# The first load of a fused cross-attention kernel as two DMAs of 64 partitions, issued by SyncE and by ScalarE

## What is computed

```python
B, C1, C2, N = (8, 512, 512, 1024)
D = C2 // 8
q = jnp.einsum('bcn,dc->bnd', x1, Wq) + bq
k = jnp.einsum('bcn,dc->bdn', x2, Wk) + bk[:, None]
v = jnp.einsum('bcn,dc->bdn', x2, Wv) + bv[:, None]
attn = jax.nn.softmax(jnp.einsum('bnd,bdm->bnm', q, k), axis=2)
attn_out = jnp.einsum('bcm,bnm->bcn', v, attn)
return attn_out + x1
```

## Time and profile before

| What | Value |
|---|---|
| Device time, median of 3 runs | 642.52 us (642.16 to 642.61) |
| Device time of the profiled execution | 642.35 us |
| Its span, first to last instruction | 640.6 us |
| Around the span | 1.75 us |
| Busy: PE, PEld, DVE, ACT, POOL | 636.6, 522.3, 461.2, 342.1, 120.6 us |
| DMA traffic | 100.11 MB, all but a few packets on SP's queue |

### The profile page before, as it was taken

The page is one execution under the profiler, slowest core; times in us unless marked ns, Lnnn a source line. Parts: engine busy times, 40 slices in busy tenths (PEclk is TensorE's granted clock), DMA queues, the critical chain, the costliest instruction groups (busy, mean ns, idle before and its releaser), DMA issues.

```text
span 640.6 us, 9766 instructions
## 1 busy us (share of the span) xinstructions
PE 636.6 (99%) x3522; PEld 522.3 (82%) x3522; DVE 461.2 (72%) x533; ACT 342.1 (53%) x451; POOL 120.6 (19%) x58
## 2 busy tenths in 40 slices
PE   9999999999999999999999999999999999999998
PEld 7888888888888888888888888888888888888886
DVE  6996769847698477994678946888558886498441
ACT  6786546734457445475455653555626647276120
POOL 0343100530006300062000620006200152002100
PEclk9999999999999999999999999999999999999999
DMA  8634435862267732776328753287442963434442
GB/s 339 200 135 102 127 105 146 308 171 87 90 166 278 180 95 69 189 266 168 98 65 220 255 147 101 79 232 249 126 126 73 257 224 106 131 94 119 109 146 73
DMA packets 40063, 100.11 MB, mean 156 GB/s; under 512 B 7280, under 2 KB 7536, under 8 KB 40048
## 3 DMA queue, kind: packets, MB, share of 16 engines
q1 hardware_dynamic: 40048, 99.91, 51.9%
HBM read 51.64 MB, written 16.78 MB: 107 GB/s over the span
## 4 chain that ended last, share of the span: by engine, by line
PE 99%; DMA 1%; DVE 0%; issue 0%
PE acc_ps L1154 43%; PE acc_ps L1132 15%; PE acc_ps L1185 10%; PE acc_ps L1122 9%; PE s_ps L1072 8%; PE s_ps L1088 7%; PE acc_ps L1335 2%; PE acc_ps L1320 1%; PE acc_ps L1203 1%; PE s_ps L1311 1%; DMA pt_raw<-in_head_dram 1%; PE acc_ps L1169 1%; PE acc_ps L1326 0%; PE acc_ps L1305 0%; PE s_ps L1080 0%; PE s_ps L1081 0%
## 5 line engine op out<-in xcount | busy, mean ns | idle before, releaser
L1154 PE MATMUL acc_ps<-pt_hi,vt_hi 128*128 128x512 f32 x408 | 158.9, 390 | 0.0
L1154 PE MATMUL acc_ps<-pt_hi,vt_lo 128*128 128x512 f32 x408 | 158.8, 389 | 0.0
L1154 PE MATMUL acc_ps<-pt_lo,vt_hi 128*128 128x512 f32 x408 | 158.8, 389 | 0.0
L362 POOL TENSOR_TENSOR pt_lo<-pt_raw,pt_hi 128x1024 fp32r<-128x1024 f32 x14 | 39.6, 2826 | 361.3 <-ACT pt_hi L426 361.3
L1154 PEld LDWEIGHTS acc_ps<-pt_hi,vt_hi 128*128 128x128 f32 x408 | 76.6, 188 | 16.2 <-issue 0.4
L1154 PEld LDWEIGHTS acc_ps<-pt_lo,vt_hi 128*128 128x128 f32 x408 | 76.6, 188 | 15.9
L1154 PEld LDWEIGHTS acc_ps<-pt_hi,vt_lo 128*128 128x128 f32 x408 | 76.6, 188 | 15.8
L776 DVE TENSOR_REDUCE negmax<-s_ps 128x1 f32<-128x1024 f32 x64 | 77.5, 1213 | 16.7 <-PE s_ps L1090 15.9
L362 POOL TENSOR_TENSOR xs_lo<-stage,xs_hi 128x1024 fp32r<-128x1024 f32 x29 | 71.9, 2501 | 82.0 <-ACT xs_hi L426 82.0
L525 ACT ACTIVATE probs<-s_ps,negmax 128x1024 f32<-128x1024 f32 x56 | 62.5, 1117 | 44.1 <-DVE negmax L776 43.6
L426 ACT ACTIVATE pt_hi<-pt_raw 128x1024 fp32r<-128x1024 f32 x60 | 61.9, 1057 | 27.3 <-PE acc_ps L1154 26.3
(11 more groups left out here) (173 smaller groups left out, 1422.1 us busy)
## 6 DMA issues: line engine op xcount, KB each, us to landing
pt_raw<-blocks SPq DMA_DIRECT2D x240, 128.0 KB, 2.3
stage<-in_x_dram SPq DMA_DIRECT2D x32, 512.0 KB, 6.8
o_sb<-in_x_dram SPq DMA_DIRECT2D x64, 256.0 KB, 3.4
out_dram<-o_sb SPq DMA_DIRECT2D x63, 256.0 KB, 2.4
stage<-in_ctx_dram SPq DMA_DIRECT2D x28, 512.0 KB, 9.1
pt_raw<-in_head_dram SPq DMA_DIRECT2D x4, 512.0 KB, 5.7
stage<-in_tail_dram SPq DMA_DIRECT2D x2, 512.0 KB, 7.4
v_sum<-in_wkq_dram SPq DMA_DIRECT2D x1, 256.0 KB, 4.9
```

What stands on the lines that cost most here:

```text
L362: return nc.gpsimd.tensor_tensor(out, src, hi.bitcast(F32), ALU.subtract)
L1154: mm = nc.tensor.matmul(acc_ps[:, out_bank(c, first), :], v[:, m, cols], p[:, m, :], start=(m == 0 and v is vt_hi and p is pt_hi), stop=(m ...
```

## The change

The first load, `head(0)`, becomes two DMAs. SP issues the one for partitions 0 to 63, ACT the one for partitions 64 to 127, as the first instruction of its own program. Both add 16 to the same semaphore, and the two engines that read the tile, ACT and DVE, wait for 32 in place of 16. All else stays.

```diff
@@ block.sync
-            head(0)
+            sp.dma_start(heads[0:D, 0, :], head_d[0, 0:D, :]).then_inc(s_head[0], 16)
             head(1)
             sp.dma_start(v_sum[:], wkq_d).then_inc(s_wkq, 16)
             tail(0)
@@ block.scalar
-            act.wait_ge(s_head[0], 16)
+            nc.scalar.dma_start(heads[D:2 * D, 0, :], head_d[0, D:2 * D, :]).then_inc(s_head[0], 16)
+            act.wait_ge(s_head[0], 2 * 16)
             copy(wv_hi[:, 0, 0:C // 2], wv_raw[:, 0, 0:C // 2]).then_inc(s_wvhi, 1)
             copy(xs_hi[:, 0, P:NH], head_raw[:, 0, P:NH]).then_inc(s_headhi, 1)
@@ block.vector
             def first_hi():
-                dve.wait_ge(s_head[0], 16)
+                dve.wait_ge(s_head[0], 2 * 16)
```

## The result

The changed kernel takes 643.63 us (median of 9 runs, 643.37 to 645.16) against 642.73 us for the kernel before (9 runs, 642.16 to 643.07). The ratio, which takes in all the runs, is 1.0023 with a 95% interval of 1.0015 to 1.0031; the medians alone differ by 0.14%. So the change is slower, by about the 0.2% that the prediction called detectable, and its time lies outside the predicted range, which ended at 643.3.

The account below looks back on a forecast made before the run. PE bounds the kernel, busy 636.6 of 640.6 us, so its start on real data sets the end. SP's half, ACT's half, table load, shared queues and waits each added 0: 642.5 us, range 642.0 to 643.3.

Parts of the forecast that it names:

- the rival that put it first: ACT's opening: table load stays ahead of ACT's issue, half lands 1.28 us late, 643.8 us or more; chance 0.09.
- ACT's half: First load: ACT's added issue moves the last byte by -0.10 to +0.34 us; value taken 0.
- two queues on the same engines: First load on the DMA engines: both queues served in turn, the second half ends when the single load ended; 0.
- one behind the other: First load: ACT's DMA is prepared after SP's and comes 0.43 us later, 642.95 us; chance 0.17.
- matmuls further apart only beside a clock under 1.00: PE behind its first real matmul: a sign that would show the forecast wrong; no size given.
- two floors: PE's start: at most 0.26 us earlier because of the zero matmuls, 0.18 us because of POOL's copy of k.

Follow-up runs that it names:

- two column halves, switch on: The changed kernel with halves cut by columns over all 128 partitions, `nc.dge_precook` left on, against the kernel before: 642.84 us, ratio 1.0006.
- the same, switch off: Column halves of 128 partitions issued by SP and ACT, with `nc.dge_precook` turned off for both loads: 642.90 us in its one run.

## Why the prediction was wrong

The sum of the delay, from the profiles of the kernels with one semaphore (us; "last packet" is the start of the last of the tile's closing packets):

| Kernel | last packet | tile complete | between | DVE starts | adds |
|---|---|---|---|---|---|
| one load (before) | 3.79 | 4.21 | 0.42 | 4.23 | |
| two column halves, switch on | 3.84 | 4.36 | 0.52 | 4.39 | 0.16 |
| the same, switch off | 4.46 | 4.77 | 0.31 | 4.79 | 0.40 |
| two halves of 64 partitions (the change) | 4.34 | 5.28 | 0.94 | 5.30 | 0.51 |

So the delay of 1.07 us has two parts of nearly equal size: the bytes end 0.55 us later, and the landing comes another 0.52 us later behind them. The first is about what the column halves lose with the switch off (0.67 us in their row), with the same issue times and ACT's bytes first. That it has the same cause in the 64-partition halves is my estimate from these numbers: no run turns the switch for them. The second comes with the cut into blocks of partitions: it isn't there with the column halves, switch on or off, nor with even and odd partitions, and it is there in every profile of the 64-partition halves (0.77 us and more) and, smaller, at the cut at 96. Single profiles differ by 0.2 us and more in the time of the bytes, so the first part is good to no more than that; the second is well outside its spread (0.94 to 1.02 in the change and its relatives).

**Right.** PE's start sets the end, one for one: 1.07 us later at the start, 1.0 in the span. No other wait of PE appeared. The table load stood behind the issue and was hidden, so the rival that put it first didn't happen. Where it did come late, in the kernels with two waits, its 1.28 us stood on the path as that rival said.

**Wrong: the term "ACT's half", -0.10 to +0.34 us, and "two queues on the same engines", 0.** They are the term that was mis-sized, and it measures +1.07. Three assumptions went into it. The issue was taken from a load of 128 partitions, 0.43 us; it is 0.56 to 0.59. The halves were to be served in turn; SP's first byte came 0.9 us behind ACT's. And the bounds were those of the issue alone. The prediction had counted 2.1 us outside the transfer, "the issue, the wait for the first byte and the report of the last one", and then let only the first of the three move. All three moved: alone, the first byte comes 1.37 and 1.78 us after the start of the issue for the halves of 64 partitions, against 1.02 and 0.97 for column halves with the switch on, and the report of the last one takes 0.94 us in the change against 0.42. The rival "one behind the other" had a part of the mechanism, with the order reversed (SP's half was the late one) and 0.43 us as its price; the late report, half of the delay, is in no rival.

**The row I should have read** is one of the moves between partitions. Besides two biases of a few bytes they are the only transfers of the kernel before that take a part of the partitions. It is the same in both kernels; here from the one after (ns, min/median/max):

```profile
L290 SPq DMA_DIRECT2D pt_raw<-blocks x240: 507/591/1940, 56.1 to 609.6; - x120
```

I bounded the issue by a store over all 128 partitions, 0.33 us, and by a bias of a few bytes, 0.77, and centred it on the loads, 0.43. The nearest row in shape says 0.59 for 32 partitions with 128 KB, half the bytes of a 64-partition half. It would have given the issue (0.56 to 0.59), but neither of the two larger parts.

**Wrong: the clock's part.** The clock column reads 1.00, and the prediction names matmuls further apart only beside a clock under 1.00, among what would show it wrong. That column can't be read so at the start, as shown at the end of this document. The one room its sums leave for a slower PE is the "or more" of the table-load rival, which neither a row nor a run gives a size there; the runs showed 1.5 us. With a gap of 1.3 us, three runs of nine cost 1.5 us more. It is an amount above the 1.0 us, not a separate case, and should have widened the upper end for every way in which the load lands late.

What stays open: why the halves of 64 partitions are issued in 0.56 to 0.59 us with the switch on, like column halves with it off (0.55 to 0.60), when 96 and 32 partitions take 0.40 and 0.33, why the landing of a block of partitions comes so late behind its last packet, and why SP's bytes come behind ACT's though its issue starts 0.01 us earlier. In 4.0 to 4.4 us SP's packets of the changed kernel also took nearly twice as long for their bytes (0.08 MB fill the engines to 98.5%, against 0.16 MB at 107% before); why isn't known.

No version beat both kernels. The whole tile alone on the engines landed 0.2 us sooner in its one profile, but by the prediction's two floors, 0.26 and 0.18 us, there is too little to win for a measurement to show it.

## What to carry to other kernels

Where an engine is busy to the end, the first load is paid one for one (here 1.07 us at PE's start, 1.0 us in the span), and splitting it in two is a gamble on the times before the first byte and behind the last, which half the size didn't halve here: alone they were 1.03 and 0.36 us for the whole tile, 1.02 and 0.35 for the first column half, 1.37 and 0.77 for the first half of 64 partitions. If it must be split, cut it by columns over all 128 partitions (complete at 4.36 us here, against 4.82 for the cut at 96 and 5.28 for the change). Look at the issue's duration (the column halves took 0.34 to 0.40 us with the switch on and 0.49 to 0.60 with it off, and the first byte, 0.36 and 0.46 us later, was late by more than the difference), and look at the time from the last packet to the landing as well. Price a new DMA from the row nearest in shape, not in size, and when a start slips by a microsecond, reckon with what PE does after the longer gap (1.5 us more in three runs of nine here).

## What the runs showed of the hardware

- The time from the start of the issue to the first byte isn't a constant. Alone on one queue it was 1.02 and 0.97 us for loads of 128 partitions by 2 KB with the switch on, 1.38 and 1.43 with it off, and 1.37 and 1.78 for 64 partitions by 4 KB.
- Nor is the time from the last packet to the landing. Alone it was 0.29 to 0.36 us for the whole tile and for column halves, switch on or off, but 0.77 and 0.82 for blocks of 64 partitions, 0.47 to 0.50 for one of 96 and 0.62 to 0.63 for one of 32. With two queues it was 0.29 us for the later half of the even and odd partitions and 0.94 for that of the two blocks.
- Of two issues started within 0.01 us, ACT's had its first packet at 2.1 us and SP's at 3.0 to 3.1, in both assignments of the 64-partition halves, and at 2.1 and 2.9 for the column halves with the switch off. With it on the column halves did mix, both queues moving 0.06 to 0.09 MB in each 0.4 us from 2.4 to 3.2.
- After a gap of 0.6 to 1.6 us PE went on at half rate in some executions and not in others: in the profiles with both halves on SP's queue (a gap of 1.49 us) and with the halves exchanged (1.28) its first four matmuls took 2.05 and 2.04 us, in those of the change (1.32) and of five zero matmuls (0.63) 1.30 and 1.29. With a gap of 0.4 us none of the 22 runs of two kernels was on the upper level. The clock column reads 1.00 all the same in the exchanged halves' profile, where each microsecond holds four matmuls in place of six:

```profile
7.00:8.00 1.00, 1.00 (x4) 1.00 1.02 406
8.00:9.00 1.00, 1.00 (x4) 1.00 0.99 397
```

In the profile with a semaphore for each half, four in a microsecond stand beside 0.50 and six beside 1.00. So the 1.00 at the opening is no measurement, and the spacing of the matmuls must be read beside it. Nor did PE need to fall in the gap, as the zeros themselves ran slowly. The changed kernel has eight records of zeros, the next two lines are those with five and with six zero matmuls:

```profile
0.78 4.61 PE L1361 MATMUL s_ps<-const-float32-0.0 128*128 128x256 f32 x10 [0.78 <-PEq L1449]
0.78 5.16 PE L1361 MATMUL s_ps<-const-float32-0.0 128*128 128x256 f32 x12 [0.78 <-PEq L1449]
```

The fifth adds 0.86 us to the 3.75, the sixth only 0.55. So the rate rises during the sixth, near 5.5 us. Read so, the lower level of times are executions in which it rises before the real work or soon after its start, the upper level those in which it rises some 3 to 4 us later, as near 9 us with both halves on SP's queue and near 10 with the halves exchanged. What makes it rise late wasn't tested further.
- A second semaphore wait ahead of ACT's first copy moved its table load behind a wait: 1.28 us at 5.39 in place of 0.74 before and 1.34 in the change.
